# Flamingo block on one core: third pair's value products and totals made neighbours, sixth head's maximum subtracted by GpSimd

## The reference, cut to what matters

```python
xn = layernorm(x, gm, bm); ln = layernorm(latents, gl, bl)
q = ln @ Wq;  k, v = jnp.split(jnp.concatenate([xn, ln], axis=-2) @ Wkv, 2, axis=-1)
sim = jnp.einsum('bhid,bhjd->bhij', q / scale, k)
sim = sim - jax.lax.stop_gradient(jnp.max(sim, axis=-1, keepdims=True))
attn = jax.nn.softmax(sim, axis=-1)
out = jnp.einsum('bhij,bhjd->bhid', attn, v)      # then @ Wout
x = x + jnp.tanh(g_xattn[0]) * out
x = x + jnp.tanh(g_ffn[0]) * ffn(layernorm(x))
```

## Time and profile before

| | |
|---|---|
| median of 3 runs | 1051.58 us (1051.32 to 1052.86) |
| profiled execution | span 1050.2 us from first to last instruction; the page gives no other time of that execution |
| PE busy | 1032.4 us, 98% of the span, 6940 matmuls |
| PEld busy | 842.3 us, 80% |
| DVE busy | 792.4 us, 75% |
| ACT busy | 593.0 us, 56% |
| POOL busy | 314.6 us, 30% |
| granted TensorE clock, mean | 0.998 of full speed |

### The profile page before, as it was taken

The page is one execution under the profiler, slowest core; times in us unless marked ns, Lnnn a source line. Parts: engine busy times, 40 slices in busy tenths (PEclk is TensorE's granted clock), DMA queues, the critical chain, the costliest instruction groups (busy, mean ns, idle before and its releaser), DMA issues.

```text
span 1050.2 us, 19053 instructions
## 1 busy us (share of the span) xinstructions
PE 1032.4 (98%) x6940; PEld 842.3 (80%) x6940; DVE 792.4 (75%) x1228; ACT 593.0 (56%) x1147; POOL 314.6 (30%) x289
## 2 busy tenths in 40 slices
PE   5999999999999999999999999999999999999997
PEld 4878778877877877887787787777788888998887
DVE  6488879987987987998798798779434555585766
ACT  6558547656654854765665485467446433455435
POOL 5333633335434363333543436334000000000000
PEclk9999999999999999999999999999999999999999
DMA  6302010100201201010020200122530000201011
GB/s 196 135 1 75 5 36 23 53 6 28 76 0 35 75 1 35 23 53 8 27 76 0 75 0 0 35 86 58 157 120 21 1 1 29 93 2 41 21 61 42
DMA packets 31907, 47.43 MB, mean 45 GB/s; under 512 B 2300, under 2 KB 11532, under 8 KB 31868
## 3 DMA queue, kind: packets, MB, share of 16 engines
q1 hardware_dynamic: 31732, 46.74, 13.8%
q10 hardware_dynamic: 136, 0.17, 0.1%
HBM read 39.56 MB, written 7.34 MB: 45 GB/s over the span
## 4 chain that ended last, share of the span: by engine, by line
PE 96%; DVE 2%; DMA 1%; ACT 1%; issue 0%; SPq 0%; DVEq 0%; ACTq 0%
PE work L491 42%; PE work L644 14%; PE score L657 13%; PE heads_out L596 9%; PE score L570 9%; PE score L506 2%; PE heads_out L608 1%; PE score L861 1%; DMA vals<-in_L_xattn_Wkv 1%; PE maxes L583 1%; PE heads_out L491 1%; DVE on L1457 0%; PE maxes L578 0%; PE maxes L596 0%; PE score L777 0%
## 5 line engine op out<-in xcount | busy, mean ns | idle before, releaser
L1882 POOL TENSOR_TENSOR dsum<-dsum,probs 125x448 f32<-125x448 f32 x186 | 221.1, 1189 | 14.6
L491 PE MATMUL work<-wv,xT 128*125 128x512 f32 (+1 forms) x768 | 187.0, 397 | 0.0
L491 PE MATMUL work<-xT,wk 128*128 128x486 f32 (+2 forms) x756 | 181.7, 390 | 1.5 <-DVE xT L1506 1.0
L491 PEld LDWEIGHTS work<-wv,xT 128*125 128x125 f32 (+1 forms) x768 | 137.9, 183 | 37.4 <-issue 2.3
L644 PE MATMUL work<-zT,wf 128*128 128x512 f32 (+1 forms) x768 | 164.1, 364 | 0.0
L491 PEld LDWEIGHTS work<-xT,wk 128*128 128x128 f32 x756 | 137.9, 188 | 31.0 <-issue 4.6
L644 PEld LDWEIGHTS work<-zT,wf 128*128 128x128 f32 x768 | 131.5, 189 | 23.0 <-issue 0.7
L999 ACT ACTIVATE probs<-score 125x448 f32<-125x448 f32 (+1 forms) x256 | 119.8, 548 | 46.2 <-PE score L570 46.2
L1879 POOL TENSOR_TENSOR dsum<-probs 125x448 f32<-125x448 f32 x31 | 41.0, 1322 | 340.2 <-ACT probs L1005 340.2
L1410 DVE TENSOR_TENSOR probs<-probs,maxes 125x1792 f32<-125x1792 f32 x64 | 128.4, 2016 | 1.1
L657 PE MATMUL score<-hT,wp 128*128 128x512 f32 (+1 forms) x576 | 117.4, 354 | 0.0
(11 more groups left out here) (207 smaller groups left out, 1447.8 us busy)
## 6 DMA issues: line engine op xcount, KB each, us to landing
xin<-in_ctx SPq DMA_DIRECT2D x42, 250.0 KB
neuron<-in_L_ffn_W_fc SPq DMA_DIRECT2D x16, 256.0 KB, 3.1
neuron<-in_L_ffn_W_proj SPq DMA_DIRECT2D x16, 256.0 KB, 3.0
xres<-in_x SPq DMA_DIRECT2D x16, 224.0 KB, 2.6
x_scratch<-xres SPq DMA_DIRECT2D x16, 224.0 KB, 2.5
xin<-in_x SPq DMA_DIRECT2D x14, 224.0 KB, 9.9
zt<-x_scratch SPq DMA_DIRECT2D x3, 1024.0 KB, 6.5
fin<-x_scratch SPq DMA_DIRECT2D x3, 1024.0 KB, 5.7
```

The lines of the kernel that those rows point to most:

```text
L491: mm = pe.matmul(bank, lhs(i, k), rhs(j, k), start=(n == 0), stop=(n == len(passes) * chunks - 1))
L1882: pool.tensor_tensor(total[0:ROWS[t]], total[0:ROWS[t]], tile(t), ALU.add).then_inc(dchain if t < TILES - 1 else dsum_done, 1)
```

## The change

Two things are moved. On PE, `attend(b, 2)` goes from in front of `keys_queries(b + 1, 1, (1,))` to behind `max_rows(b, 3)`, and `totals(b, 2)` from behind `scores(b + 1, 0, 0)` to right behind `attend(b, 2)`. In the loop, `subtract(b, 5)` is taken off DVE; POOL does it as `subtract_fifth(b)` between `denominators(b, 1)` and `denominators(b, 2)`. Since POOL can't reach PSUM, `row_maxima` of pair 2 now writes its rows into `mx` in SBUF in place of `maxes`, and `subtract(b, 4)` on DVE reads them from there too. `maxima(b, 3)`, which overwrites `mx`, waits for POOL's subtraction (`fifth_sub`), and so does `exponentials(b, 5)` on ACT; in ACT's list `copy_scores(b, 3, 3)` moves in front of `exponentials(b, 5)`. The last batch element keeps its order and its DVE subtractions.

```diff
+        FIFTH = 5
+        def subtracted(h, last):
+            return h + 1 if last or h < FIFTH else h
+        def maxima_rows(p, last):
+            return mx[:, :, :].rearrange("p e l -> p (e l)") if p == FIFTH // 2 and not last else maxes[:, 0:2 * L]
...
                 keys_queries(b + 1, 1, (0,))
-                attend(b, 2)
                 keys_queries(b + 1, 1, (1,))
                 max_transposes(b, 3)
                 keys_queries(b + 1, 1, (2,))
                 max_rows(b, 3)
+                attend(b, 2)
+                totals(b, 2)
                 scores(b + 1, 0, 0)
-                totals(b, 2)
...
-            def exponentials(b, h):
-                act.wait_ge(sub_done, b * HEADS + (h + 1))
+            def exponentials(b, h, last=False):
+                if h == FIFTH and not last:
+                    act.wait_ge(fifth_sub, b + 1)
+                else:
+                    act.wait_ge(sub_done, b * (HEADS - 1) + subtracted(h, last))
...
-                copy_scores(b, 3, 2)
+                copy_scores(b, 3, 2, 3)
                 exponentials(b, 5)
-                copy_scores(b, 3, 3)
...
                 dve.wait_ge(top_done, n * FOLDS + FOLDS)
+                if p == 3:
+                    dve.wait_ge(fifth_sub, b + 1 if not last else b)
                 dve.tensor_tensor(mx[:, :, :], top[:, :, 0:L], top[:, :, L:2 * L], ALU.max).then_inc(mx_done, 1)
...
-                dve.transpose(maxes[:, 0:2 * L].rearrange("p (j a) -> p j a", a=SQ), row).then_inc(mrow_done, 1)
+                dve.transpose(maxima_rows(p, last).rearrange("p (j a) -> p j a", a=SQ), row).then_inc(mrow_done, 1)
...
-                row = maxes[0:CT, e * L:(e + 1) * L].rearrange("p (o l) -> p o l", o=1)
+                row = maxima_rows(h // 2, last)[0:CT, e * L:(e + 1) * L].rearrange("p (o l) -> p o l", o=1)
...
                 folds(b, 3, 1)
-                subtract(b, 5)
                 kq_lo_parts(b + 1, 0, 1)
...
+            def subtract_fifth(b):
+                pool.wait_ge(mrow_done, b * PAIRS + (FIFTH // 2 + 1))
+                v = probs[0:CT, FIFTH % 4, :].rearrange("p (t l) -> p t l", t=TILES)
+                row = maxima_rows(FIFTH // 2, False)[0:CT, L:2 * L].rearrange("p (o l) -> p o l", o=1)
+                pool.tensor_tensor(v, v, row.to_broadcast([CT, TILES, L]), ALU.subtract).then_inc(fifth_sub, 1)
...
+                if not last:
+                    subtract_fifth(b)
                 denominators(b, 2)
```

More of the change, by code:

```diff
@@ L280, in flamingo_block @@
         sub_done = sem("sub_done")
+        fifth_sub = sem("fifth_sub")
         exp_done = sem("exp_done")
@@ L1136, in last_batch @@
                 copy_values(b, 3)
-                exponentials(b, 1)
+                exponentials(b, 1, last=True)
                 copy_values(b, 4, 5)
@@ L1140, in last_batch @@
                 group_variances(0)
-                exponentials(b, 2)
-                exponentials(b, 3)
+                exponentials(b, 2, last=True)
+                exponentials(b, 3, last=True)
                 group_norm(0)
@@ L1155, in last_batch @@
                 split_weights(3)
-                exponentials(b, 4)
-                exponentials(b, 5)
+                exponentials(b, 4, last=True)
+                exponentials(b, 5, last=True)
                 heads_hi(b, 1)
@@ L1161, in last_batch @@
                 squares(0, 0)
-                exponentials(b, 6)
+                exponentials(b, 6, last=True)
                 relus(0, 2)
                 split_weights(5)
-                exponentials(b, 7)
+                exponentials(b, 7, last=True)
                 squares(0, 1)
@@ L1375, in folds, with maxima @@
                                           ALU.max).then_inc(top_done, 1)
-            def maxima(b, p):
+            def maxima(b, p, last=False):
                 n = b * PAIRS + p
@@ L1394, in query_maxima, with row_maxima, subtract @@
                                   ALU.max).then_inc(qmax_done, 1)
-            def row_maxima(b, p):
+            def row_maxima(b, p, last):
                 dve.wait_ge(mxb_mm, b * PAIRS + (p + 1))
                 row = maxes[:, 2 * L:2 * L + QB].rearrange("p (j o) -> p j o", o=1).to_broadcast([P, QB, SQ])
-                dve.transpose(maxes[:, 0:2 * L].rearrange("p (j a) -> p j a", a=SQ), row).then_inc(mrow_done, 1)
-            def subtract(b, h):
+                dve.transpose(maxima_rows(p, last).rearrange("p (j a) -> p j a", a=SQ), row).then_inc(mrow_done, 1)
+            def subtract(b, h, last=False):
                 if h % 2 == 0:
-                    row_maxima(b, h // 2)
+                    row_maxima(b, h // 2, last)
                     dve.wait_ge(mrow_done, b * PAIRS + (h // 2 + 1))
@@ L1550, in last_batch @@
                 group_moments(0)
-                subtract(b, 2)
+                subtract(b, 2, last=True)
                 kq_lo_parts(b, 2, 2)
-                subtract(b, 3)
+                subtract(b, 3, last=True)
                 latent_values(b, 6)
@@ L1564, in last_batch @@
                 group_lo(0, 0, 1, 2, 3)
-                subtract(b, 4)
-                subtract(b, 5)
+                subtract(b, 4, last=True)
+                subtract(b, 5, last=True)
                 folds(b, 3, 1)
@@ L1569, in last_batch @@
                 folds(b, 3, 2, 3)
-                maxima(b, 3)
+                maxima(b, 3, last=True)
                 query_maxima(b, 3)
                 split_weights(4)
-                subtract(b, 6)
+                subtract(b, 6, last=True)
                 heads_lo(b, 1)
-                subtract(b, 7)
+                subtract(b, 7, last=True)
                 h_lo_part(0, 0)
```

## The result

| | before | changed |
|---|---|---|
| median of 18 runs each | 1051.45 us | 1053.74 us |
| ratio, 95% interval | | 1.0020 (1.0014 to 1.0027) |
| span of the profiled execution | 1050.2 us | 1051.5 us |
| PE / DVE / ACT / POOL busy | 1032.4 / 792.4 / 593.0 / 314.6 | 1031.3 / 774.1 / 590.8 / 355.6 |

A forecast was written before the change was run, and what follows sets the result against it. PE was taken to bound the kernel, with 96% of the chain. Per 7 loop passes, order on PE -1.0, stall +3.7, POOL 0 gave +2.7 us: 1054.3 us, 0.26% slower, range 1050.6 to 1059.5.

The forecast's parts named there:

- the cover: Value products on PE hid DVE's stretch from maxima(b, 3) to the fourth low part; moving them takes that away.
- The order on PE: Value products followed directly by totals cost 0.09 + 0.05 = 0.14 us less; 7 times, -1.0 us.
- The stall: PE waits ahead of KQ(1, 2) for DVE's fourth low part: 0.53 us, 7 times, +3.7 us; bounds 0.45 to 1.19.
- The estimate of 4.1 us from two sizes: POOL's subtraction of 1792 elements, from 1.15 us for 448 and 1.29 for 512, at 2.2 ns per further element.
- the cover held: POOL's denominators end at 377.7, PE wants them at 378.5; with 0.8 us to spare POOL's work costs 0.
- The rule of the Trainium skill: DVE with two SBUF inputs and GpSimd reading SBUF exclude each other per instruction; read on starts, DVE goes first.
- Third rival: POOL's subtraction goes first, DVE's subtract(b, 4) ends 4.0 us later, PE stalls in the scores: +30 us, 1081; 12%.
- First rival: No stall ahead of KQ(1, 2), DVE gives back enough; only the new order counts: -1.0 us, 1050.6; 17%.
- The second: Rival: POOL's move changes nothing as ACT is later anyway, DVE's list not shorter where it counts: +1.5, 1053.1; 6%.
- The fourth: Rival: POOL's subtraction takes 6 us or more, denominators come late, PE waits 0.8 at the totals: +13, 1064; 5%.
- The range: 1050.6, the first rival's time, to 1059.5, the upper end of the stall's bounds; leaves out third and fourth rival.
- the other 0.3: Added to the stall's bounds if `mx<-top` on DVE meets POOL's adds at a worse moment.

The follow-up runs named there:

- POOL first: Changed kernel with a one-element copy ahead of DVE's subtraction, so DVE starts behind POOL: 1084.5 us with a wait for the copy, 1085.05 without.
- no blocking: Changed kernel with the maxima's rows written twice, PSUM for DVE's subtraction and SBUF for POOL's: 1057.13 us, ratio 1.0061.
- the two kernels with the copy: Changed kernel with a one-element copy ahead of DVE's subtract(b, 4), with and without a wait for it: 1084.5 and 1085.05 us.
- the kernel without the wait: Changed kernel with a one-element copy ahead of DVE's subtract(b, 4), and no wait for that copy: 1085.05 us, ratio 1.0321.

## Why the prediction was right, point by point

- **Total.** Forecast 1054.3, +2.7 us; measured 1053.74, +2.3 us, and +2.7 in the loop. The mechanism came as told: the cover is gone, and a hole opens ahead of KQ(1, 2) with the fourth low part as its releaser. That the number fits so well is luck in part: 0.39 a pass was forecast and 0.38 measured, but both terms of it are too small, by 0.20 and by 0.18, and the errors cancel.
- **The order on PE.** -0.14 a pass was forecast, -0.34 measured. The step that was short is "what PE pays for a piece is start to start", read from one neighbourhood: KQ(1, 0) and KQ(1, 1) side by side cost 5.31 undisturbed, while apart, with value products between, they cost 5.54. The entry from `max_rows` into the value products, which I had left open, is 0.23, as into the scores.
- **The stall.** 0.53 was forecast, 0.71 measured: 0.60 ahead of KQ(1, 2), and 0.11 at the transpose, which the forecast had at nothing ("finds `rmax` at 373.05, in time"). The low part and `rmax` were placed to 0.02 (the low part at 373.69, which is 373.52 on the changed kernel's clock, where that place of the loop comes 0.17 earlier; measured 373.50); PE was ready 0.23 earlier than I had it, the same 0.23 as in the term before, and the hand-over took 0.05, not 0.08. Undoing POOL's part raised the waits to 1.39, and letting DVE do `normalise` early closed the hole: so the cause is shown, not only argued.
- **POOL.** The estimate of 4.1 us from two sizes is borne out by 4.05 (POOL first) and 4.08 (no blocking). DVE went first, by 0.04 us, and the cover held: the denominators were 0.9 early (0.8 forecast).
- **The rule of the Trainium skill** ("SBUF — State Buffer", "Who interferes with whom"): the trace agrees that one side waits for the whole instruction of the other, in either direction, 3.9 us for DVE and 1.8 for POOL. That issue order decides agrees with the recorded starts of this pair, at a lead of 0.04 and at a lag of 0.03; it does not agree with the recorded starts of two other pairs, which the last section has.
- **Third rival.** Its price, +30 us, was measured as +33 by forcing it, though by another way: 3.3 us of hole as forecast (3.5), but the last 1.6 us a pass by a slower clock and not by a second hole. Its chance of 12% stood on a margin of 0.04 us. One argument against it was not read from the starts: the first add of 1903 ns was given as a case where "DVE came before", but in its record POOL starts 0.27 us before DVE (last section).
- **First rival.** That no stall would be left fell: of the 1.92 us freed, 1.09 turned into idle time of DVE, for ACT's high part and for the totals; 0.16 went because an instruction that waits doesn't overlap the one before it, as it did by 0.08 twice in the earlier trace rows; and 0.67 reached the fourth low part (0.66 forecast). The second fell with it: DVE's list was shorter where it counts. The fourth didn't come; POOL needed 4.1 us of its own, not 6. Its price of +13 counts the stall twice: with PE 0.66 later at KQ(1, 2), it would ask for the totals 0.66 later too and wait some 0.25 there and not 0.8, which makes +9.
- **The range.** Its upper end, 1059.5, is not what its bounds give: a stall of 1.19 gives 1058.9, with the other 0.3 it is 1061.0. The measured time lies far from either.

## What to carry to other kernels

On an engine that is never idle, work that is moved away from a place was also the cover of what is awaited behind that place: list what each piece behind it waits for, and by how much it was early, before moving it. Help for another engine counts only up to the next thing that this engine itself waits for; here 1.9 us freed became 0.7. And where two engines exclude each other and it matters who goes first, one semaphore should not start both: here it hung on 0.04 us, and the wrong one costs 3%.

## What the runs showed of the hardware that I had not expected

- For the two subtractions the order between DVE and POOL turns over between a lead of 0.04 us for DVE and a lag of 0.03, without exception in 7 passes each. For other pairs the recorded starts don't tell it. A case in the earlier trace rows went the other way at a lead of 0.04, with an operation that also reads a per-partition operand. And in the changed kernel a first add of POOL starts 0.27 us before DVE's last fold, of the same kind as the subtractions, and yet waits it out, 1.90 us in place of 1.15, while the fold keeps its 0.62 (timelines of POOL and DVE; 7 times, in the kernel before too):

```profile
146.01 1.90 POOL L1893 TENSOR_TENSOR dsum<-probs 125x448 f32<-125x448 f32 x1 [15.55 <-ACT probs L1019]
```

```profile
146.28 0.62 DVE L1397 TENSOR_TENSOR mx<-top 128x448 f32<-128x448 f32 x1
```

DVE has no idle time ahead of that fold, as it had none between the copy and the subtraction, which lost. What tells these cases apart stays open.

- After each hole of 3.3 us in the two kernels with the copy TensorE's granted clock reads 0.50 for some 3.5 us, its level of 1.2 GHz in place of 2.4, and the pieces cost 1.6 us more. The clock was at full level through the hole itself and fell 0.3 to 1.1 us after the work came back. One of the 14 holes is an exception, the first of the kernel without the wait: there it fell 1.4 us before the end of the hole, stayed low for nearly 7 us, and the same pieces cost 2.3 us more. After holes of 0.6 and 1.2 us no piece was slower.
